# Vision tower on one core: expert channels in blocks of 128 and 64, up products two blocks ahead of down products

## What is computed

```
def _moe(x, r_w, r_b, fc_w, fc_b, proj_w, proj_b):
    scores = x @ r_w + r_b
    gate = jax.nn.softmax(jnp.mean(scores, axis=1), axis=-1)
    vals, idx = jax.lax.top_k(gate, TOP_K)
    hmid = _gelu(jnp.einsum('bnd,edf->benf', x, fc_w) + fc_b[None, :, None, :])
    outs = jnp.einsum('benf,efd->bend', hmid, proj_w) + proj_b[None, :, None, :]
    k_outs = jnp.take_along_axis(outs, idx[:, :, None, None], axis=1)
    return jnp.sum(vals[:, :, None, None] * k_outs, axis=1)
...
x = _layernorm_global(a + x, ln1_w, ln1_b)
m = _moe(x, r_w, r_b, fc_w, fc_b, proj_w, proj_b)
x = _layernorm_global(m + x, ln2_w, ln2_b)
```

## Time and profile before

| | us |
|---|---|
| median of 3 runs | 1060.96 (1058.73 to 1065.21) |
| profiled execution, its own time | 1052.88 |
| its span, first to last instruction | 1051.1 |
| TensorE busy | 926.8 (88%) |
| VectorE busy | 711.2 (68%) |
| ScalarE busy | 659.5 (63%) |
| mean granted TensorE clock | 0.948 |

### The profile page before, as it was taken

The page is one execution under the profiler, slowest core; times in us unless marked ns, Lnnn a source line. Parts: engine busy times, 40 slices in busy tenths (PEclk is TensorE's granted clock), DMA queues, the critical chain, the costliest instruction groups (busy, mean ns, idle before and its releaser), DMA issues. The chain is left out here.

```text
span 1051.1 us, 20397 instructions
## 1 busy us (share of the span) xinstructions
PE 926.8 (88%) x6627; PEld 819.6 (78%) x6627; DVE 711.2 (68%) x1659; ACT 659.5 (63%) x1196; POOL 145.2 (14%) x206
## 2 busy tenths in 40 slices
PE   5999999999978897889788978897878884999996
PEld 5999999999966776677666766775777763899996
DVE  7899979989553875497449754874754436475555
ACT  5767757758535886687569756875544323566652
POOL 1000000000010334034303430333300000000000
PEclk9999999999977899999999999999788996999997
DMA  8003001099604783477237824781301113413101
GB/s 259 22 21 94 36 31 35 20 154 148 91 26 141 224 248 85 122 235 246 71 121 235 245 72 121 228 247 53 96 1 31 31 46 90 122 49 97 49 0 60
DMA packets 81691, 113.02 MB, mean 108 GB/s; under 512 B 10685, under 2 KB 42570, under 8 KB 81626
## 3 DMA queue, kind: packets, MB, share of 16 engines
q1 hardware_dynamic: 81626, 112.26, 39.2%
HBM read 61.40 MB, written 47.67 MB: 104 GB/s over the span
## 5 line engine op out<-in xcount | busy, mean ns | idle before, releaser
L399 PE MATMUL psum<-w,feat 128*128 128x192 f32 x960 | 167.9, 330 | 13.7 <-ACT feat L329 10.2
L399 PEld LDWEIGHTS psum<-w,feat 128*128 128x128 f32 x960 | 156.5, 192 | 14.6 <-issue 10.1
L614 POOL TENSOR_SCALAR a_scores<-a_scores,a_inv 112x514 f32<-112x514 f32 (+1 forms) x160 | 112.6, 704 | 290.9 <-DVE a_inv L963 290.6
L948 DVE CUSTOM_DVE_ANT_0 a_scores<-psum,a_bias 112x514 f32<-112x514 f32 (+1 forms) x160 | 109.7, 688 | 48.3 <-PE psum L687 41.9
L836 ACT ACTIVATE a_scores<-a_scores,a_least 112x514 f32<-112x514 f32 (+1 forms) x160 | 116.6, 729 | 13.8 <-DVE a_least L948 13.1
L417 PE MATMUL psum<-w_parts,parts 128*128 128x384 f32 x368 | 113.9, 374 | 2.5 <-DVE parts L231 2.3
L700 PE MATMUL psum<-ident,a_scores 112*112 112x112 f32 (+1 forms) x800 | 102.4, 260 | 14.0 <-DVE a_probsT L958 8.9
L329 ACT ACTIVATE feat<-turn 128x1024 f32<-128x1024 f32 (+1 forms) x60 | 58.5, 974 | 85.2 <-DVE turn L214 53.9
L687 PE MATMUL psum<-a_kh,a_q 128*112 128x258 f32 (+1 forms) x320 | 101.2, 337 | 6.8 <-DVE a_q L918 4.1
L700 PEld LDWEIGHTS psum<-ident,a_scores 112*112 112x112 f32 (+1 forms) x800 | 77.8, 137 | 35.3 <-POOL a_scores L614 18.3
L641 PE MATMUL psum<-h1T,place 96*128 (+3 forms) x320 | 86.9, 411 | 13.3 <-DVEq L911 6.9
(11 more groups left out here) (271 smaller groups left out, 1745.2 us busy)
## 6 DMA issues: line engine op xcount, KB each, us to landing
shear<-a_pos SPq DMA_DIRECT2D x128, 224.9 KB, 3.7
a_bias<-shear SPq DMA_DIRECT2D x128, 224.4 KB, 3.8
shear<-zero SPq DMA_DIRECT2D x20, 448.9 KB, 15.7
e_fc<-in_e_fc_dram SPq DMA_DIRECT2D x16, 336.0 KB, 4.4
x<-in_xT_dram SPq DMA_DIRECT2D x20, 256.0 KB, 2.9
e_proj<-in_e_proj_dram SPq DMA_DIRECT2D x8, 576.0 KB, 5.4
shear<-a_pos SPq DMA_DIRECT2D x32, 130.5 KB
a_bias<-shear SPq DMA_DIRECT2D x32, 130.3 KB
```

Of the source, the lines that this page charges most:

```text
L399: mm = pe.matmul(sums[m][:, 0:D], feat[:, r, j, 0, 128 * m:128 * m + 128], w[:, k, :], start=begins, stop=ends)
L614: pool.tensor_scalar(row, row, inv[0:TILES[g % NT][1], g % TT:g % TT + 1], 1.0, ALU.mult, ALU.mult).then_inc(weighed, 1)
L948: dve.tensor_tensor_reduce(halves(scores[0:r, g % TT, 0:PADL]), psum2(score_pair(g), r), halves(bias[0:r, g % MR, :]), -1.0 / 8, BIG, ALU. ...
```

## The change

The channels in `yT` stand in `BLOCKS`: 128 on all partitions, then 64. In the second block the operands are filled up: the up weights `fc_stack` have the high part on rows 0 to 63 and the low part on rows 64 to 127, and x stands twice, so that one matmul gives high and low weights times one part of x. The down weights `proj_stack` have high columns 0 to 63 and low columns 64 to 127; the sum of the two halves is formed as they are added to yT. An up item and a down item are 2 windows x (3 + 2) = 10 matmuls each.

TensorE's list is written out for all 8 passes, with up items ahead of down items by two and more. The other two engines' lists follow it: the next pass's weights are split between the items, and a pass's result is added in the next pass, behind item 1. The fc bias is a column in the Gelu (`fb`, new small loads), the router's bias an addition. The global norm sums the two blocks in two matmuls each. In the tail, out products have 128 columns and the bias of the mix goes into a ScalarE copy.

```diff
+BLOCKS = ((0, 128), (128, 64))
...
     def tensor(self, pe):
-        pe.matmul(self.m_ps.rearrange("p (c b) -> p c b", c=2), self.s.mean_w[:, :], self.means, start=True, stop=True).then_inc(self.mean_done, 1)
+        for c, (_, n) in enumerate(BLOCKS):
+            mm = pe.matmul(self.m_ps, self.s.mean_w[0:n, :], self.means[0:n, c, :], start=c == 0, stop=c == 1)
+        mm.then_inc(self.mean_done, 1)
...
+                if b == 0:
+                    sp.dma_start(fb[:, b, k], s.d["e_fcb"][bass.ds(e, 1)].rearrange("e p c -> (e p) c")).then_inc(fb_first_in, 16)
...
-            with pe.Fori(0, B) as b:
-                pe.wait_ge(x_lo, b + 1)
-                for k in range(TOPK):
-                    pe.wait_ge(w_lo, (b * TOPK + k) * 3 + 1)
-                    for m in range(HC):
...
-                        for w in range(2):
-                            for n, (pw, px) in enumerate(TERMS):
-                                for c in range(2):
-                                    mm = pe.matmul(s.bank[2 * (m % 2) + w][:, 0:WIDE],
-                                                   fc_parts[0:DC + c, k, pw, c, 128 * m:128 * m + 128],
-                                                   x[0:DC + c, px, c, w * HALF:w * HALF + WIDE],
-                                                   start=n == c == 0, stop=n == 2 and c == 1)
...
+            def up(n):
...
+                if n >= 2:
+                    pe.wait_ge(gelu_done, n - 1)
+                cols = slice(128 * m, 128 * m + 128)
+                for w in range(2):
+                    out, tokens = s.bank[UP[n % 2][w]][:, 0:WIDE], slice(w * HALF, w * HALF + WIDE)
+                    for t, (pw, px) in enumerate(TERMS):
+                        pe.matmul(out, fc_parts[:, k, pw, cols], x[:, b % 2, px, 0, tokens], start=t == 0, stop=False)
+                    for px in range(2):
+                        mm = pe.matmul(out, fc_stack[:, k, cols], x[:, b % 2, px, 1, tokens], start=False, stop=px == 1)
+                mm.then_inc(up_done, 1)
+
+            def down(n):
+                b, k, m = split(n)
+                if m == 0:
+                    pe.wait_ge(w_lo, 3 * (n // HC) + 3)
+                    if n:
+                        pe.wait_ge(added, 3 * (n // HC))
+                pe.wait_ge(hidden_lo, n + 1)
+                for w in range(2):
+                    tokens = slice(w * HALF, w * HALF + WIDE)
+                    for t, (pw, ph) in enumerate(TERMS):
+                        pe.matmul(s.bank[OUT[0][w]][:, 0:WIDE], proj_parts[:, k, pw, m, :], hidden[:, ph, m, tokens],
+                                  start=m == t == 0, stop=m == HC - 1 and t == 2)
+                    for ph in range(2):
+                        mm = pe.matmul(s.bank[OUT[1][w]][:, 0:WIDE], proj_stack[:, k, m, :], hidden[:, ph, m, tokens],
+                                       start=m == ph == 0, stop=m == HC - 1 and ph == 1)
+                mm.then_inc(down_done, 1)
...
+            for p in range(PASSES):
+                n = p * HC
+                up(n + 2)
+                up(n + 3)
+                down(n)
+                up(n + 4)
+                down(n + 1)
+                up(n + 5)
+                down(n + 2)
+                down(n + 3)
+                if p + 1 < PASSES:
+                    up(n + 6)
+                down(n + 4)
+                if p + 1 < PASSES:
+                    up(n + 7)
+                down(n + 5)
...
+            def split_fc(p, part):
...
+                act.copy(fc_parts[:, k, 0, cols], fc[:, k, 0, cols])
+                act.copy(fc_stack[:, k, cols], fc[:, k, 1, cols]).then_inc(w_hi, 1)
...
+                act.activation(halves(whole[:, n % GB, :]), psum2(UP[n % 2]), ACT.Gelu_apprx_tanh,
+                               bias=fb[:, b, k, m:m + 1]).then_inc(gelu_done, 1)
...
+            def add_out(p):
+                b, k = divmod(p, TOPK)
+                dve.wait_ge(based, 2 * b + 2)
+                dve.wait_ge(down_done, (p + 1) * HC)
+                for i, (c, rows) in enumerate(((0, slice(0, 128)), (1, slice(0, 64)), (1, slice(64, 128)))):
...
+                    dve.scalar_tensor_tensor(out=y, in0=s.psum[rows, OUT[c][0]:OUT[c][0] + 2, 0:HALF], scalar=gates[0:n, b, k:k + 1], in1=y,
+                                             op0=ALU.mult, op1=ALU.add).then_inc(added, 1)
...
+            for p in range(1, PASSES):
+                b, k = divmod(p, TOPK)
+                more = p + 1 < PASSES
+                for m in range(HC):
+                    item(p * HC + m)
+                    if more and m < 2:
+                        split_fc(p + 1, m)
+                    if m == 1:
+                        add_out(p - 1)
+                    if m in (2, 3) and k == 0:
+                        statistics(b - 1, m - 2)
+                    if more and m == 2 and k == TOPK - 1:
+                        split_image(b + 1)
+                    if more and m == 3:
+                        split_proj(p + 1)
```

More of the change, by code:

```diff
@@ L2040, in _ @@
             dve.wait_ge(weighed, 2)
+            split_fc(1, 0)
+            item(2)
+            split_fc(1, 1)
+            item(3)
             add_biases(0)
-            for b in range(B):
-                image(b, b < B - 1)
+            item(4)
+            split_proj(1)
+            item(5)
+            for p in range(1, PASSES):
+                b, k = divmod(p, TOPK)
+                more = p + 1 < PASSES
+                for m in range(HC):
+                    item(p * HC + m)
+                    if more and m < 2:
+                        split_fc(p + 1, m)
+                    if m == 1:
[4 more added lines that the diff above has]
+                        split_image(b + 1)
+                    if more and m == 3:
+                        split_proj(p + 1)
+                    if more and m == 4 and k == TOPK - 1:
+                        add_biases(b + 1)
+            add_out(PASSES - 1)
+            statistics(B - 1, 0)
+            statistics(B - 1, 1)
             dve.wait_ge(aggregated, 2 * B)
@@ L2055, in output_phase @@
         block = ctx.enter_context(nc.Block(no_gpsimd_drain=True))
-        where = [(b, j) for b in range(B) for j in range(2)]
+        where = [(b, w) for b in range(B) for w in range(2)]
         @block.vector
```

430 lines of the change are left out of this document (222 added, 208 removed).

## The result

The changed kernel takes 1072.67 us (median of 15 runs, 1067.72 to 1081.71), the kernel before 1060.96 us (15 runs beside them): a ratio of 1.0137, 95% interval 1.0111 to 1.0162. It is slower by 11.7 us, outside the range of the prediction. Its profiled execution took 1081.47 us (span 1079.6). A second timing of the same kernel gave 1068.52 us, a ratio of 1.0077 (1.0038 to 1.0115), so the loss is near 1%. Medians take every execution; ratios leave out the few that took over 1.5% more than the fastest of their kernel.

A forecast was written before the change was run, and what follows sets the result against it. The prediction took TensorE as the bound from the experts' second pass on. Its terms, -22.1 + 12.5 + 0 + 2.2 + 1.3 + 0.3 + 5.1 = -0.7 us, gave 1060 us, range 1044 to 1068.

The forecast's parts named there:

- The items: Experts' part: each up or down item takes TensorE 1.23 us, at 122.8 ns a product.
- The waits: Experts' part: TensorE waits for VectorE's output adds, 1.95 us at passes 1 to 6, 0.8 at pass 7, together +12.5 us.
- The end: After the last down product: one and a half more adds and a second statistics block on VectorE, +2.2 us.
- Up(n+4): Experts' part: program order keeps this ready up item behind the waiting down(n); passing would cut the waits by 8.2 us.
- the removal: Experts' part: ten matmuls an item instead of twelve, 2.76 us less a pass, -22.1 us over 8 passes.
- The start: First pass: biases land later, but TensorE loses 4.3 us against 4.6 before; taken as 0, bounds -2 and +3.
- The norms: Two global norms: four more small matmul groups of two records, about 0.3 us each, +1.3 us.
- The clock: Experts' part: three falls to half speed after the start's and passes' waits, 1.7 us each, +5.1 us, bounds 0 and 11.9.
- Rivals A and B: At pass boundaries: A, wait near zero, 1042.7 us, chance 0.13; B, 0.8 us a pass, 1049.9 us, chance 0.10.
- rival C: Experts' part: the lower clock lasts longer after each of seven waits, 23.8 us instead of 5.1, 1079 us, chance 0.08.
- Only the experts' part changes much, so only its waits matter: Whole kernel: the opening step, which limited the study of TensorE's waits to the experts' part; no size given.
- its last image: Tail: a bias in two ScalarE copies and two one-column matmuls for the last image, estimated at +0.3 us.

The follow-up runs named there:

- experiment 3: Changed kernel with VectorE's add of the last pass's output placed after the pass's first item, not its second: 1056.63 us, ratio 0.9977.
- experiment 4: Kernel before with one of the twelve products of each up and each down item left out: 1036.08 us, ratio 0.9786.
- experiments 1 and 2: Changed kernel with full 128 rows in the second block's output transposes: 1067.77 us; changed kernel with transposes ordered 128, 128, 64, 64 rows: transposes 8.26 us.
- experiment 6: Tail's value bias handling added to the kernel before: 1063.53 us; value bias left out of the changed kernel: 1062.15 us, tail 149.5 us.
- the kernel with both edits: Changed kernel with full rows in output transposes and in the norms' and router's small products, and VectorE's output add earlier: 1052.67 us, again 1048.90 us.
- experiment 7: The kernel with both edits, with the tail's value bias worked out on VectorE instead of by one-column products: 1046.44 and 1045.80 us.

## Why the prediction was wrong

**Right: the experts' part.** The items, twelve to a pass: forecast 1.23 us, measured 14.65/12 = 1.22. The waits: 1.95 forecast at passes 1 to 6 and 0.8 at pass 7, measured 2.07 to 2.10 and 0.81, in sum 13.3 against 12.5, and by the mechanism named, as experiment 3 shows. The end: 2.2 forecast, 4.64 - 2.63 = 2.0 measured. Up(n+4) did not pass the waiting product: nothing ran on TensorE in those 2 us, so the rule of program order from the Trainium skill ("TensorE: Matmul & The Clock Gate", "Step-by-step: what each phase is for") agrees with the trace. Of the removal, -22.1 forecast, (17.50 - 14.65) x 8 = -22.8 measured, and -24.1 by itself in experiment 4.

**Off in size.** The start: 0 forecast, 1.6 measured. From the first up product to the first wait TensorE had 16 items, 19.5 us of work, and 25.7 us passed (916.80 to 944.61 less the wait): 6.2 lost against 4.6; the first nine microseconds of it ran at half clock, before the first four. The norms: +1.3 forecast for both, by 0.3 a group; the four groups grew by 0.6 each at half clock (0.46 to 1.07 or 1.08, 0.49 to 1.10), and the router's scores, with no term, by 0.5: 2.9 in sum. The clock: three falls forecast (+5.1); in the five profiles with these waits there were one, one, two, three and three, and none in that of experiment 3, which has no waits. In sum the part came out at -1.5 us, where the terms that concern it add to -1.0. That this is so close is partly luck: start and norms were 3.2 us too low, the clock in this profile 3.4 too high. Rivals A and B are refuted by the waits; C's price did not fall due at the new waits.

**Wrong: the step "Only the experts' part changes much, so only its waits matter".** Two parts outside it carry the whole loss.

- The output transposes had no term at all. As many instructions on the same bytes looked like no change; the phase is 5.5 us longer, and experiments 1 and 2 tie it to the changes of the row count. The prediction had weighed the loads' columns (96 or 128), not what two neighbouring loads do to each other.
- The tail had +0.3 for "its last image", for which I had counted two extra instructions. They stand on the chain of all four images, 0.3 us each, 1.2 us; the tail became 14.4 us longer. The tail is, but for the short output phase, the part of the kernel in which TensorE waits most (119.15 of 144.30 us busy before), its clock at 0.89. With a few tenths more on the chain went a fall of 13.7 us, about 6 us of time, and in ten executions without the bias the time at half clock is 19 us lower by the median. I had given the clock's falls a term and a rival, but put both in the experts' part, where TensorE is busy without a break but for the new waits, and none in the tail, where it falls already before the change.

By the experiments' times the bill of 36 us reads, with the changed kernel's 24 executions taken together (1071.9): waits at the passes 16 (with a fall of the clock), the bias in the tail 10, the output's rows 4 to 5, and by the rows the end 2.0, the norms and scores 2.9, the start 1.6: 37. The first three are differences of medians, each uncertain by 3 to 5 us, so that the sum fits this well is no proof. What the tail has beyond the bias (5.2 us in experiment 6's profile) is in no line of it.

So the kernel came out slower, for which the prediction had 0.08, by two things: the row changes in the output phase, which no rival has, and the clock, which rival C has, but in another place.

**Open.** The fall in the tail is tied to the bias on the chain by four profiles without and six with it, but the bias added to the kernel before brought no such fall (tail 149.2), and the kernel with both edits had it in one of two profiles. So the bias makes it likely together with something else of the tail's change (128 columns in its loads are a candidate that wasn't tried), and why the clock falls there is not shown. With the bias off the chain the tail is still 2.6 to 5.2 us longer than before (146.9 to 149.5 against 144.3; the tail before rests on two profiles, the other 145.2). In the profile at 149.5 the clock can account for it, with 41.0 us at half clock against 31.4. In the first profile of experiment 7 (146.9) it can't, with 30.7; in the second there is a stretch of 3.4 us at clock 0.51 in its last products, where the kernel before was at full clock. The remainder isn't attributed.

## What to carry to other kernels

A change of layout is paid wherever the layout is read: list every instruction that touches the tensor, also in phases whose code looks the same, and read their rows. If blocks of unequal height are stationary operands, pad the small one to full rows or group equal ones; alternating cost TensorE its overlap of loading and multiplying here. Look also at where a drain of PSUM stands in the draining engine's order before giving up a schedule: moving one call was worth 16 us here. And a profile of one execution can sit at the edge of its kernel's range: the mean clock of every execution says more about what a change does to the clock.

## What the runs showed of the hardware

TensorE's weight loads overlapped the running transposes when neighbours had equal rows, and stopped doing so when the row count changed between them, by 0.19 us a change at 1.2 GHz (31 and 15 changes, the same instructions: 11.31 and 8.26 us). It goes both ways: idle time stands before the loads of 64 rows (0.22 us) and before those of 128 (0.12).

The Trainium skill ("TensorE: Matmul & The Clock Gate", "Step-by-step: what each phase is for") says that a load is pulled ahead if row groups don't conflict or if it goes to the background weight buffer, and that the row count doesn't matter for its time. The loads' own length agrees (181 ns with 128 rows, 179 with 64), but loads of 128 rows behind 128 rows are hidden and loads of 64 behind 128 are not, which those sentences would not lead one to expect.

Padding to full rows is cheap in this place, but not free: at half clock 32 transposes that write 128 columns each start 0.21 us apart (about 7.0 us in all, an estimate from that pace), where 32 of 96 rows and columns started 0.16 apart (5.59 us).

The granted clock at one place can be the same in two executions of a kernel (tails of 158.7 and 158.8 us) or not (the fall ahead of image 3's gram, once there and once missing), so one profile does not tell a kernel's cost of the clock.
